# Split gate and up products in a fused vision, linear attention and expert kernel, and a new order between its two halves

## The reference

```python
x = layernorm(h).reshape(-1, 256)
logits = x @ gate_w.T                      # 8 experts
top_v, sel = max(logits), argmax(logits)
rw = sigmoid(top_v)
for e in range(8):
    xs = x * (rw * (sel == e))[:, None]
    g, u = xs @ w_gate[e].T, xs @ w_up[e].T        # 256 -> 128 each
    out = out + u * silu(g) @ w_down[e].T          # 128 -> 256
return h + out
```

## Time and profile before

| what | us |
|---|---|
| median of 3 runs | 449.73 |
| lowest and highest | 447.07, 450.03 |
| the profiled execution | 450.51 |
| its span, first to last instruction | 448.7 |
| TensorE busy | 424.7 |
| GpSimd busy | 290.3 |
| VectorE busy | 327.5 |
| ScalarE busy | 278.7 |

### The profile page before, as it was taken

One profiled execution on the slowest core, in us unless ns is written; L12 is line 12 of the kernel. 1 busy time (PEld: TensorE's weight loads), 2 busy tenths in 40 slices (PEclk: granted clock), 3 DMA queues, 4 the chain that ended last, 5 costly groups with the idle time before them and its releaser, 6 DMA issues.

```text
span 448.7 us, 12774 instructions
## 1 busy us (share of the span) xinstructions
PE 424.7 (95%) x4197; PEld 402.8 (90%) x4197; DVE 327.5 (73%) x1115; ACT 278.7 (62%) x672; POOL 290.3 (65%) x662
## 2 busy tenths in 40 slices
PE   7999999999999999999999999999689999999990
PEld 7999899999999999999999999998678888888870
DVE  5578468999999999999999999988555434343440
ACT  5445476787786877877877867776425544444430
POOL 3065214688788887887887877775557766565662
PEclk9999999999999999999999999999879999999996
DMA  8974122324323121133121121077132982221120
GB/s 269 333 236 142 51 49 59 92 83 118 93 66 91 60 78 56 39 108 96 38 66 44 39 67 56 22 212 216 44 116 88 289 262 82 83 73 67 69 74 14
DMA packets 34147, 46.43 MB, mean 103 GB/s; under 512 B 8843, under 2 KB 25857, under 8 KB 34083
## 3 DMA queue, kind: packets, MB, share of 16 engines
q1 hardware_dynamic: 24860, 30.50, 22.6%
q0 software_dynamic: 9216, 15.12, 10.7%
q10 hardware_dynamic: 6, 0.00, 0.0%
HBM read 26.87 MB, written 17.17 MB: 98 GB/s over the span
## 4 chain that ended last, share of the span: by engine, by line
PE 82%; DVE 6%; issue 4%; DMA 3%; ACT 2%; POOL 1%; POOLq 0%; SPq 0%; DVEq 0%
PE b_kg L1608 11%; PE b_w L1347 7%; PE b_w L1348 6%; PE b_w L1349 6%; PE b_att L1462 6%; PE b_kg L1347 4%; PE b_kg L1349 4%; PE b_kg L1348 4%; PE b_t L1412 3%; DMA rows_all<-in_x 3%; PE b_v L1349 3%; PE b_v L1347 3%; PE b_v L1348 3%; PE b_att L1644 3%; PE b_w L1644 3%
## 5 line engine op out<-in xcount | busy, mean ns | idle before, releaser
L662 POOL DMA_INDIRECT sorted_rows<-rows,place x64 | 75.4, 1178 | 20.3 <-issue 9.7
L740 POOL DMA_INDIRECT out<-result,rows_all x64 | 62.4, 975 | 36.5 <-DVE result L1277 24.4
L1608 PE MATMUL b_kg<-wgu,xsT 128*128 x256 | 67.2, 386 | 0.1
L1266 DVE SCALAR_TENSOR_TENSOR act_u<-b_kg,rows_all,silu_g 128x128 f32<-128x128 f32 x64 | 19.5, 346 | 58.1 <-ACT silu_g L933 58.1
L846 ACT ACTIVATE q_exp<-b_w,bq_s 128x228 f32<-128x228 f32 x64 | 28.9, 452 | 33.1 <-PE b_w L1349 33.1
L1608 PEld LDWEIGHTS b_kg<-wgu,xsT 128*128 128x128 f32 x256 | 44.4, 193 | 4.0 <-issue 0.2
L1347 PE MATMUL b_w<-xnT_hi,wq_hi 128*128 128x264 f32 x128 | 39.3, 307 | 1.3 <-DVE logits L1088 1.0
L1347 PE MATMUL b_kg<-wkgv_hi,xnT_hi 128*114 128x264 f32 x128 | 38.7, 302 | 0.4 <-DVE patch_out L1005 0.4
L1462 PE MATMUL b_att<-kv_sb,qT 128*114 128x136 f32 x256 | 35.4, 282 | 1.9 <-issue 1.9
L1348 PE MATMUL b_kg<-wkgv_lo,xnT_hi 128*114 128x264 f32 x128 | 36.4, 284 | 0.0
L1349 PE MATMUL b_kg<-wkgv_hi,xnT_lo 128*114 128x264 f32 x128 | 36.4, 284 | 0.0
(11 more groups left out here) (225 smaller groups left out, 1439.0 us busy)
## 6 DMA issues: line engine op xcount, KB each, us to landing
rows_all<-sorted_rows SPq DMA_DIRECT2D x64, 130.0 KB, 2.5
rows_all<-in_x SPq DMA_DIRECT2D x18, 384.0 KB, 4.9
rows_all<-in_txt SPq DMA_DIRECT2D x32, 154.0 KB
wgu<-in_wgu_in SPq DMA_DIRECT2D x8, 256.0 KB, 3.0
rows_all<-patch_out SPq DMA_DIRECT2D x48, 36.0 KB
sorted_rows<-tail_rows SPq DMA_DIRECT2D x9, 130.0 KB, 2.2
sorted_rows<-rows,place POOLq DMA_INDIRECT x64, 3.7
wdown<-in_wdown_in SPq DMA_DIRECT2D x2, 512.0 KB, 5.0
```

The costliest lines, as they stand in the source:

```text
L662: G.indirect_dma_start(out=scratch[0:EXPERTS * REGION, :], out_offset=bass.IndirectOffsetOnAxis(ap=place[:, k, b:b + 1], axis=0), in_=rows ...
L740: G.indirect_dma_start(out=out, out_offset=bass.IndirectOffsetOnAxis(ap=rows_all[:, t.n, ID:ID + 1].bitcast(I32), axis=0), in_=result[:, k ...
L1266: last = V.scalar_tensor_tensor(act_u[:, t.slot(4)], b_gu[m.slot(2)][:, up:up + INNER], rows_all[:, t.n, GAIN:GAIN + 1], silu_g[:, t.slot( ...
L1608: last = T.matmul(to, xsT[:, t.slot(6), k, :], wgu[:, bass.ds(e, 1), k, :], start=(k == 0), stop=(k == KC - 1))
```

## The change

- `wgu` becomes `wgu_hi` and `wgu_lo`. SyncE now loads an expert's weights raw into rows of `rows_all` that pairs 0 to 7 have left (after a wait on `h2_ready`). In the steps 10 to 25 ScalarE rounds one half of an expert's weights in each step (`gate_up_high`, 128x256, ahead of its `queries(i)`), and GpSimd subtracts (`gate_up_low`, 128x256, at the end of its step): 16 of each.
- `gate_up` makes three split matmuls for each of its two float32 ones: 6 for a tile. `xsT` becomes `xsT_hi` (the ScalarE copy, rounding) and `xsT_lo` (a new VectorE instruction `rows_low`, 128x512, for each duo).
- The order between the halves is new on all engines. TensorE begins duos 0, 1 and 2 among the last two pairs; `load_experts(0)` comes after two turns, and `load_experts(1)` with duo 4. VectorE makes `queries(31)` ahead of `attention_low(30)`. GpSimd counts pair 31 only after it has scattered pair 30. ScalarE's silu and copies of duos 0 to 2 stand among the last `centred` and `tanh`.
- The ring of results grows from 8 to 16 tiles, and for the first three duos the turned activations and the down products use `b_w` alone.

The core of the diff:

```diff
+            def gate_up_low(n):
+                e, k = divmod(n, KC)
+                pool.wait_ge(gu_hi_done, n + 1)
+                G.tensor_tensor(wgu_lo[:, e, k, :], gate_up_raw(e)[:, k, :], wgu_hi[:, e, k, :].bitcast(F32), ALU.subtract).then_inc(gu_lo_done, 1)
...
+            def gate_up_high(n):
+                e, k = divmod(n, KC)
+                act.wait_ge(s_expert_w[e], 16)
+                S.copy(wgu_hi[:, e, k, :], gate_up_raw(e)[:, k, :]).then_inc(gu_hi_done, 1)
...
+            def rows_low(m):
+                dve.wait_ge(xsT_hi_ready, m.upto())
+                low(duo(xsT_lo, m, 3).rearrange("p t k n -> p (t k n)"), b_x[m.slot(2)],
+                    duo(xsT_hi, m, 3).rearrange("p t k n -> p (t k n)")).then_inc(xsT_lo_ready, 1)
...
             count_chosen(PAIRS - 2)
             scatter(PAIRS - 3)
-            count_chosen(PAIRS - 1)
             rstd2_of(PAIRS - 2)
             top_value(PAIRS - 2)
+            scatter(PAIRS - 2)
+            count_chosen(PAIRS - 1)
             rstd2_of(PAIRS - 1)
-            scatter(PAIRS - 2)
             top_value(PAIRS - 1)
             scatter(PAIRS - 1)
...
                 for k in range(KC):
-                    last = T.matmul(to, xsT[:, t.slot(6), k, :], wgu[:, bass.ds(e, 1), k, :], start=(k == 0), stop=(k == KC - 1))
+                    last = product(to, (xsT_hi[:, t.slot(6), k, :], xsT_lo[:, t.slot(6), k, :]),
+                                   (wgu_hi[:, bass.ds(e, 1), k, :], wgu_lo[:, bass.ds(e, 1), k, :]), k == 0, k == KC - 1)
...
             rank(PAIRS - 4)
             key_value(PAIRS - 1)
+            turn_attention(PAIRS - 2)
+            turn_rows(Turn(0, 0))
             load_experts(0)
-            turn_attention(PAIRS - 2)
             apply(PAIRS - 1)
             project_out(PAIRS - 2)
-            load_experts(1)
+            turn_rows(Turn(0, 1))
+            first_products(Turn(0, 0))
+            gate_up(Turn(0, 0), 0)
+            turn_attention(PAIRS - 1)
+            gate_up(Turn(0, 0), 1).then_inc(gu_done, 1)
             rank(PAIRS - 3)
-            turn_attention(PAIRS - 1)
-            duo_step(Turn(0, -2))
+            turn_rows(Turn(0, 2))
+            first_products(Turn(0, 1))
+            gate_up(Turn(0, 1), 0)
+            turn_act(Turn(0, 0))
+            gate_up(Turn(0, 1), 1).then_inc(gu_done, 1)
             rank(PAIRS - 2)
             project_out(PAIRS - 1)
-            duo_step(Turn(0, -1))
+            down(Turn(0, 0))
+            turn_rows(Turn(0, 3))
+            first_products(Turn(0, 2))
+            gate_up(Turn(0, 2), 0)
+            turn_act(Turn(0, 1))
+            gate_up(Turn(0, 2), 1).then_inc(gu_done, 1)
+            down(Turn(0, 1))
             rank(PAIRS - 1)
             late_count()
-            duo_step(Turn(0, 0))
+            turn_rows(Turn(0, 4))
+            duo_step(Turn(0, 3))
             late_slots()
-            duo_step(Turn(0, 1))
-            straight(STEPS_B, duo_step)
+            straight(range(4, DUOS + 1), duo_step)
```

More of the change, by code:

```diff
@@ L305, in build @@
         s_down_w = sem("s_down_w")
-        s_expert_w = sem("s_expert_w")
+        s_expert_w = [sem(f"s_expert_w{e}") for e in range(EXPERTS)]
+        gu_hi_done = sem("gu_hi_done")
+        gu_lo_done = sem("gu_lo_done")
         s_prep = sem("s_prep")
@@ L1257, in _, with act_of @@
                 step(i)
+            def act_of(m):
+                dve.wait_ge(silu_ready, m.upto())
+                if m.had(2):
+                    dve.wait_ge(turn_a_done, m.upto(2))
+                for t in tiles_of(m):
+                    up = t.slot(2) * D + INNER
+                    last = V.scalar_tensor_tensor(act_u[:, t.slot(4)], b_gu[m.slot(2)][:, up:up + INNER], rows_all[:, t.n, GAIN:GAIN + 1],
+                                                  silu_g[:, t.slot(4)], ALU.mult, ALU.mult)
+                last.then_inc(act_ready, 1)
@@ new lines, in result_of @@
+            def result_of(m):
+                dve.wait_ge(down_done, m.upto())
+                if m.had(RESULT_RING // DUO):
+                    for t in tiles_of(m):
+                        dve.wait_ge(stored[t.slot(RESULT_RING)], 16 * t.rounds(RESULT_RING, RESULT_RING))
+                for t in tiles_of(m):
+                    at = t.slot(2) * D
+                    last = V.scalar_tensor_tensor(result[:, t.slot(RESULT_RING)], rows_all[:, t.n, 0:D], rows_all[:, t.n, MEAN:MEAN + 1],
+                                                  down_bank(m)[:, at:at + D], ALU.add, ALU.add)
+                last.then_inc(result_ready, 1)
@@ L1264, in duo_step @@
[L1264 to L1268, removed]
-                if (j - 1).within(DUOS):
[L1270 to L1279, removed]
+                    act_of(j)
@@ L1315, in _ @@
             places(PAIRS - 4)
+            queries(PAIRS - 1)
             attention_low(PAIRS - 2)
-            queries(PAIRS - 1)
             route(PAIRS - 3)
+            rows_low(Turn(0, 0))
             attention(PAIRS - 1)
@@ L1321, in _ @@
             gate_logits(PAIRS - 2)
+            route(PAIRS - 2)
+            rows_low(Turn(0, 1))
+            attention_low(PAIRS - 1)
+            act_of(Turn(0, 0))
             places(PAIRS - 3)
-            route(PAIRS - 2)
-            attention_low(PAIRS - 1)
+            rows_low(Turn(0, 2))
             stats_2(PAIRS - 2)
+            act_of(Turn(0, 1))
             residual(PAIRS - 1)
             gate_logits(PAIRS - 1)
+            result_of(Turn(0, 0))
+            route(PAIRS - 1)
+            rows_low(Turn(0, 3))
             places(PAIRS - 2)
-            route(PAIRS - 1)
+            stats_2(PAIRS - 1)
+            duo_step(Turn(0, 2))
             places(PAIRS - 1)
             late_count()
-            stats_2(PAIRS - 1)
-            duo_step(Turn(0, 0))
+            duo_step(Turn(0, 3))
             late_slots()
-            duo_step(Turn(0, 1))
+            duo_step(Turn(0, 4))
             late_rows()
-            straight(STEPS_B, duo_step)
+            straight(range(5, DUOS + 1), duo_step)
         @block.tensor
```

82 lines of the change are left out of this document (50 added, 32 removed).

## The result

The changed kernel takes 437.49 us (median of 4 runs, 436.53 to 439.06) against 449.34 for the kernel before (median of 4, 447.07 to 450.03): ratio 0.975, 95% interval 0.970 to 0.979. The profiled execution took 436.53, span 434.7. It is the fastest of its four, while the profiled execution of the kernel before (450.51) is slower than any of the four timed beside it.

The account below looks back on a forecast made before the run. TensorE was taken to bound both halves, only the passage being loose: 450.5 - 7.1 (passage) - 5.4 (periods) - 0.2 (last products) - 0 (attention) = 437.8, less 0.8 to the median: 437.0 us. Range for 8 in 10: 432.5 to 443.

Parts of the forecast that it names:

- Products and the stall: Second half: six matmuls take 0.71 us a tile; TensorE stands 0.11 before `down`; a duo's period falls from 3.25 to 3.05.
- The rival of a full gain: Second half: the 0.11 stall doesn't show and TensorE keeps its clock in the passage; 433 us, chance 0.11.
- that of no gain: Second half: issue of matmuls with register addresses sets the period at 3.25, only the passage gains; 442.5 us, chance 0.06.
- Passage: Between the halves, key-value 31 to duo 4: the new order gains 7.1 us, bounds 2 and 11.
- the walk: Passage followed, engine by engine: TensorE work 17.1 us plus waits 5.6, duo 4 8.2 earlier at full clock.
- The wait at `late_count`: Passage: TensorE waits 2.5 us for pair 31's count, which GpSimd makes behind the two DMAs of scatter 30.
- The half-clock stretch: Passage: after the 2.5 us gap TensorE runs one stretch at half clock instead of three, costing 1.1 us.
- The last products: End of the kernel, from duo 31: the last products save 0.2 us.
- The attention: First half: splitting the weights on ScalarE and GpSimd costs 0 us, bounds 0 and 5.7.
- this sign of being wrong: Attention: the forecast is wrong if its step grows in steps 10 to 25; 8.2 us was expected to stay.
- a lock each step: Attention: VectorE's `qT` and GpSimd's subtraction exclude each other each step, c 1.29, loss 10 us; 447 us, chance 0.05.
- The price line of GpSimd's rival: Attention: GpSimd sets the pace; loss 16 x (c - 0.49) - 2.5 us, 458.7 us at c = 2.0; chance 0.05.

Follow-up runs that it names:

- the split alone: The changed kernel's weight split and three matmuls per float32 one, with the order between the halves of the kernel before: 441.79 us, ratio 0.986.
- the second subtraction: The changed kernel with a second, unused GpSimd subtraction of the same size in each of the 16 attention steps: 450.89 us, ratio 1.006 to the kernel before.
- the kernel before with fillings: The kernel before with 46 unused small matmuls at four places of its passage where TensorE waits: 446.58 us, ratio 0.998.
- the variant with the early count: The changed kernel with GpSimd's count of pair 31 moved ahead of the scatter of pair 30: 437.16 us, ratio 0.977 to the kernel before.

## Why the prediction was right

437.0 was forecast and 437.49 came. Step by step:

- **Products and the stall: right.** Six products in 0.71 were foretold. Weight load to weight load they take 391.48 - 390.76 = 0.72, but by the starts of the matmuls, by which the 0.87 before was read, it is 391.58 - 390.79 = 0.79, since the second follows the first after 0.20. `turn_act` behind them gives this back (0.14 instead of 0.22), so that the first tile saves the 0.16 foretold and the second 0.04 (foretold 0.05). The stall of 0.11 behind `turn_act` was foretold, and 0.10 measured (392.51 instead of 392.41). Undoing it gave a period of 2.93 to 2.94, the lower bound named (2.94). The rival of a full gain (2.94) was out for the reason given; that of no gain (3.25) is refuted by the split alone, at 3.05.
- **Passage: right in its sum and in its largest wait, with two errors that cancel.** Duo 4 comes 7.94 us earlier relative to key-value 31; the walk had 8.2, and 7.1 with the half clock. The wait at `late_count` was foretold at 2.5 and is 2.45. The wait for apply was foretold at 0.8 and is 0.74. The copies for duo 1 and duo 2 were put at 0.7 and 0.65 and cost 0.29 each, the load of expert numbers 0.19 and not 0.4, and the waits for the low rows of duo 1 and for `act_u` of duo 0 (0.35 and 0.25) don't show. Together the waits are 4.0 us and not 5.6. TensorE's work from key-value 31 to duo 4 was put at 17.1 us and takes 335.31 - 312.29 - 3.96 = 19.1. A tile of duo 0, for one, takes 317.63 - 316.83 = 0.80 instead of 0.71. That 1.6 too much met 2.0 too little was luck.
- **What the walk missed** is that the wait hid a second one. It named a single releaser, the count; the centring of pair 31 ahead of `actT(2)` costs as much once the count is early.
- **The half-clock stretch: wrong for the profiled execution, open for the median one.** I took 1.1 for it. The profiled execution has none; where one came it cost 0.8. The mean clocks of the other executions allow a stretch and don't prove it.
- **The last products: a sign off, of no weight** (+0.16 for -0.2).
- **The attention: 0.4 instead of 0.** Its step grew from 8.23 to 8.26, so this sign of being wrong came, at a small size. Two terms failed. The subtraction takes 0.741 and not 0.671; the row that I took was on 48 partitions, and that this is the reason was not tried. And the 0.38 in `route_w` was called waiting that falls away once GpSimd is late. It was the lock with `qT`, which hits whatever GpSimd does then. It happened to shrink to 0.15 here and grew back to 0.46 with the second subtraction. The rival "a lock each step" had the right mechanism with the wrong victim and the wrong base: it put `qT`'s 0.62 on top of the subtraction, but the lock stood in the step before the change already (0.39, on an instruction of 0.2), and it became smaller with it.
- **The price line of GpSimd's rival: right in kind, within 2 us in size.** Loss = 16 x (c - 0.49) - 2.5, for a cost of c in a step. With c as the time of the instructions alone, 1.48, it gives 13.3, and the attention grew by 14.6 against before. With c read back from the step, 0.49 + 9.40 - 8.23 = 1.66, which holds the gaps and the lock too, it gives 16.2. For c = 0.74 it gives 1.5, and 0.4 came. A cost as high as that of two subtractions makes the change a loss, as that rival said: 450.89 against 448.32 for the kernel before beside it.
- **The start: put at nothing.** The profiled execution of after reaches key-value 0 1.51 us sooner than that of before. Nothing in the change stands there. In nine experiments, with the same work up to there but for one, the start took 54.9 to 56.5 us; among them is the kernel before with fillings, at 55.97. So this is the spread from one execution to the next, and the profile of before, with 57.02, lies above all the others.

So the sum of -12.7 against the profiled execution was, in its own terms, -12.5 (-7.94 - 5.17 + 0.41 + 0.16), and the early start of the other execution, which is luck, made it 14.0. Against medians the change is worth 11.9 us by the runs of its own comparison. The kernel before ran somewhat faster beside the experiments (medians 447.16, 448.32 and 447.28); the variant with the early count, whose time is that of the changed kernel, was 10.0 us faster than it there. The profiled execution of before was at the slow end of that kernel's, by its start and by the clock in its passage.

What stays open is why the start varies, where the rest of the 2.0 us more of work in the passage lies (the eight tiles explain 0.7), and what decides whether an execution gets a half-clock stretch behind a wait.

## What to carry to other kernels

When a wait comes from the order on another engine, follow what every engine does behind the releaser too: here the count and ScalarE's copy were late by the same scatter, moving one gave 0.3 us and moving both 2.7. Where a small instruction shows several times its usual length in one step out of the pattern, look whether VectorE runs an instruction with two SBUF inputs at that moment before calling it waiting. And before using a profile as the base of a sum, compare its granted clock and its first milestones with the other executions.

## What was not expected of the hardware

- The lock between VectorE and GpSimd cost the GpSimd instruction at most 0.48 us in the three traces counted above, 0.39 in the mean before, for a `qT` of 0.62. It hit instructions of 0.2 as hard as large ones (0.23 became 0.69, and two of 0.73 became 1.17 and 1.09).
- The matmuls of float32r operands with 128x128 weights and 256 columns start 0.118 us apart, loads included, also where the weights' address comes from a register (the third product at 391.11 in the kernel after, the sixth at 391.46). The first of a tile is an exception: the second follows it after 0.20.
- TensorE's weight load follows a ScalarE copy that it waits for by 0.14 us, before and after. Four independent matmuls in between hid it, with the period at 2.93 instead of 3.05.
